# The second edge list of a two-layer graph network in groups of 128 edges instead of 256

## The reference, cut to what matters

```
h_fwd, h_rev = h @ W_forward.T, h @ W_reverse.T                      # 3125 x 64
messages = h_fwd[src] * direction[:, 0:1] + h_rev[src] * direction[:, 1:2]
scores = leaky_relu(einsum('ef,hf->eh', messages, attn_forward[0]), 0.2)   # 4 heads
norm = exp(scores - max) / (segment_sum(exp(scores - max), dst)[dst] + 1e-10)
outs = [segment_sum(messages * norm[:, hd:hd + 1], dst, N) for hd in range(H)]
x = x + stack(outs) + attention(xn)        # then another graph attention with 4 experts
```

## Time and profile before

| | |
|---|---|
| median of 3 runs | 2914.25 us (2913.68 to 2917.84) |
| the profiled execution: its time / its span | 2912.84 us / 2910.9 us |
| busy share of the span: PE, DVE, ACT, POOL | 74%, 57%, 41%, 70% |
| second layer's edge sum | from 1814 us to 2435 us of the span |
| indirect DMAs in it (L2408) | 440 |
| additions of PE's sums in it (L2621) | 220 |
| mean granted TensorE clock | 0.855 |

### The profile page before, as it was taken

One profiled execution on the slowest core, in us unless ns is written; L12 is line 12 of the kernel. 1 busy time (PEld: TensorE's weight loads), 2 busy tenths in 40 slices (PEclk: granted clock), 3 DMA queues, 4 the chain that ended last, 5 costly groups with the idle time before them and its releaser, 6 DMA issues. The chain is left out here.

```text
span 2910.9 us, 34578 instructions
## 1 busy us (share of the span) xinstructions
PE 2167.6 (74%) x10021; PEld 1675.2 (58%) x10021; DVE 1673.6 (57%) x4649; ACT 1187.8 (41%) x3164; POOL 2037.0 (70%) x2064
## 2 busy tenths in 40 slices
PE   0275482277766768999999997688877776999994
PEld 0054361144444447878888876455555455888883
DVE  8937899366679885111000125788887766333236
ACT  0111354155555542222222213699954444344443
POOL 4777777677777776777777633777777773777761
PEclk9996555588888887999999999899987876999997
DMA  2020000533333341356666632322222241111111
GB/s 65 2 63 2 6 3 2 191 105 105 105 104 103 102 98 35 121 163 200 195 197 198 191 105 91 95 53 54 53 52 52 52 49 11 29 32 36 17 19 47
DMA packets 173391, 233.36 MB, mean 80 GB/s; under 512 B 59819, under 2 KB 136622, under 8 KB 172206
## 3 DMA queue, kind: packets, MB, share of 16 engines
q0 software_dynamic: 73664, 103.00, 15.6%
q1 hardware_dynamic: 96504, 117.82, 13.1%
q10 hardware_dynamic: 3062, 10.68, 1.0%
HBM read 192.31 MB, written 39.04 MB: 79 GB/s over the span
## 5 line engine op out<-in xcount | busy, mean ns | idle before, releaser
L831 POOL DMA_INDIRECT slots_gnn<-rec_gnn,slot_row_gnn x782 | 771.3, 986 | 286.4 <-issue 229.9
L2408 POOL DMA_INDIRECT arena<-table,rec_gnn x440 | 457.5, 1040 | 161.9 <-issue 124.7
L1222 POOL DMA_INDIRECT rows_gnn<-support,xT x416 | 401.2, 964 | 132.7 <-issue 110.9
L1266 PE MATMUL banks<-rows_gnn,one_hot 128*128 128x256 f32 x832 | 304.3, 483 | 199.9 <-DMA rows_gnn<-support,xT 174.9
L1266 PEld LDWEIGHTS banks<-rows_gnn,one_hot 128*128 128x128 f32 x832 | 163.1, 228 | 322.8 <-DMA rows_gnn<-support,xT 183.8
L2986 POOL DMA_INDIRECT source_rows<-table_g,source_router x256 | 245.7, 960 | 78.0 <-issue 63.1
L2507 PE MATMUL banks<-weighted,one_hot 128*128 128x260 f32 x880 | 268.7, 458 | 3.0 <-DVE weighted L2604 2.0
L1871 ACT ACTIVATE hidden_private<-banks,b_private 128x256 f32<-128x256 f32 x256 | 107.3, 470 | 354.3 <-PE banks L1829 354.3
L1829 PE MATMUL banks<-slot_xT,w_private 128*128 128x256 f32 x1024 | 228.2, 381 | 1.7 <-DVE slot_xT L1885 1.7
L1841 PE MATMUL banks<-w_private,hidden_private 128*128 128x256 f32 x1024 | 226.1, 379 | 0.0
L2507 PEld LDWEIGHTS banks<-weighted,one_hot 128*128 128x128 f32 x880 | 188.2, 224 | 61.0 <-issue 27.0
(11 more groups left out here) (576 smaller groups left out, 3976.0 us busy)
## 6 DMA issues: line engine op xcount, KB each, us to landing
w_private<-in_w1p SPq DMA_DIRECT2D x32, 1024.0 KB
w_private<-in_w2p SPq DMA_DIRECT2D x32, 1024.0 KB, 7.6
slots_gnn<-rec_gnn,slot_row_gnn POOLq DMA_INDIRECT x782, 2.1
slot_x<-zero_rows ACTq DMA_DIRECT2D x8, 1024.0 KB, 11.2
slot_rows<-slot_x SPq DMA_DIRECT2D x32, 256.0 KB, 7.0
slot_y<-slot_out SPq DMA_DIRECT2D x32, 256.0 KB, 2.2
arena<-table,rec_gnn POOLq DMA_INDIRECT x440, 2.6
rows_gnn<-support,xT POOLq DMA_INDIRECT x416, 2.7
```

Of the source, the lines that this page charges most:

```text
L831: pool.indirect_dma_start(e.slots, bass.IndirectOffsetOnAxis(e.rows[:, j:j + 1], 0), e.rec[:, j, :], None)\
L1222: pool.indirect_dma_start(e.rows_in[:, k, :], None, table, bass.IndirectOffsetOnAxis(row, 0))\
L1266: mm = pe.matmul(bank_of(k // per), hot[:, k, :], e.rows_in[:, row, :], start=k % per == 0, stop=k % per == per - 1)
L2408: pool.indirect_dma_start(c.raw[:, t % RAW_RING, :], None, c.table1, bass.IndirectOffsetOnAxis(row, 0))\
```

## The change

The second list takes groups of 128. It has 416 tiles in 52 rounds. Each tile has its own sum and its own addition: four matmuls of a half go to banks 0 to 3, each with `start` and `stop`, and the next half uses the same four banks again. A new semaphore, `tiles_added1`, counts additions. PE's matmul for tile n waits until addition n-4 is done. DVE makes eight additions a round; each waits for the one before. `add_half(i, 0)` moves up, from behind `late_dve` to directly behind `rescale`, and `scale_v` moves ahead of `add_half(i-1, 1)`. `load_tiles` reads 8 numbers every round, behind `add_half(i-1, 1)`. The attention's output takes two node tiles a round from round 29, so that it ends by round 41. The ring has 64 tiles instead of 72. The POOL part of `attend_stage` waits until all engines have met behind the table stage, not only for the stores.

```diff
-RAW_RING = 72
+RAW_RING = 64
@@ late_dve
-        elif T + 4 <= i < 2 * T + 4:
-            t = i - T - 4
-            dve.wait_ge(self.y_ready, t + 1)
+        elif i >= T + 4:
+            for t in range(2 * (i - T - 4), min(2 * (i - T - 3), T)):
+                dve.wait_ge(self.y_ready, t + 1)
@@ half_sums
             for k in range(HALF * h, HALF * h + HALF):
-                mm = pe.matmul(c.bank[:, k // per, 0:AGG], hot[:, k, :], val[:, k, :, :].rearrange("p h f -> p (h f)"),
-                               start=k % per == 0, stop=k % per == per - 1)
+                n = i * RING + k
+                if n >= HALF:
+                    pe.wait_ge(added, n - HALF + 1)
+                mm = pe.matmul(c.bank[:, k % HALF, 0:AGG], hot[:, k, :], val[:, k, :, :].rearrange("p h f -> p (h f)"),
+                               start=True, stop=True)
@@ rescale
             dve.wait_ge(step, ch.n)
+            if i:
+                dve.wait_ge(added, i * RING)
@@ add_half
             dve.wait_ge(used, 2 * i + h + 1)
-            for k in range(half_groups):
-                g = half_groups * h + k
-                dve.wait_ge(step, ch.n)
-                mark(dve.tensor_tensor(tile_of(i, g), c.bank[:, g, 0:AGG], tile_of(i, g), ALU.add))
+            for g in range(HALF * h, HALF * h + HALF):
+                if i or g:
+                    dve.wait_ge(added, i * RING + g)
+                if g == 0:
+                    dve.wait_ge(step, ch.n)
+                dve.tensor_tensor(tile_of(i, g), c.bank[:, g % HALF, 0:AGG], tile_of(i, g), ALU.add).then_inc(added, 1)
@@ DVE's round
             weigh(i, 0)
+            if 2 <= i <= T + 1:
+                mix.scale_v(dve, i - 2)
             if i:
                 add_half(i - 1, 1)
+            load_tiles(i)
             if more:
                 scaled = forward(i + 1)
-            if 2 <= i <= T + 1:
-                mix.scale_v(dve, i - 2)
-            if i % TURN == 0:
-                load_tiles(i)
             one_hots(i, 1)
@@
             rescale(i)
+            add_half(i, 0)
             if 1 <= i <= T:
                 mix.variances(dve, ch, i - 1)
@@
             mix.late_dve(dve, i)
-            add_half(i, 0)
             if more:
                 shift(i + 1)
@@ attend_stage, POOL
-        pool.wait_ge(c.table_stored, 16 * c.table_stores)
+        pool.wait_ge(met, 4 * (met_n - 1))
@@ build
-        e1 = Edges(c, "gnn1", EDGES, a["dst"], a["src"], a["edge_attr_2"], top, rounds=True)
+        e1 = Edges(c, "gnn1", EDGES, a["dst"], a["src"], a["edge_attr_2"], top, group=P, rounds=True)
```

More of the change, by code:

```diff
@@ L39 @@
 PARTS_IN_FLIGHT = FLIGHT // HALF
-BODY_GROUPS = RING * P // GROUP
+ROOM_WORDS = 1736
 NEG = -1.0e30
@@ L185, in hold_records @@
         if then_slots:
-            self.room = c.sb(ctx, f"rec_{self.name}", [P, max(self.per, self.tiles) * self.width])
+            self.room = c.sb(ctx, f"rec_{self.name}", [P, max(self.per * self.width, self.tiles * self.width, ROOM_WORDS)])
             self.rec = self.room[:, 0:self.per * self.width].rearrange("p (j w) -> p j w", w=self.width)
@@ L1185, in _ @@
           .then_inc(e.slot_in, 16)
-TURN = 3
 def tiles_of_groups(c, engine, e, first, n):
@@ L2327, in late_pe @@
             mm.then_inc(self.mat2_ready, 1)
-        elif T + 3 <= i < 2 * T + 3:
-            t = i - T - 3
-            if t == 0:
-                pe.wait_ge(self.mat2_out, 1)
-            if t >= 2:
-                pe.wait_ge(self.y_out, t - 1)
-            out = self.raw[:, t % 2, 0:D]
-            for k in range(KD):
-                pe.matmul(out, self.c.xT[:, k, t * P:(t + 1) * P], self.mat2[:, k, :], start=k == 0, stop=False)
-            pe.matmul(out, self.c.ones[0:1, 0:P], self.bo[:], start=False, stop=True).then_inc(self.y_ready, 1)
+        elif i >= T + 3:
+            for t in range(2 * (i - T - 3), min(2 * (i - T - 2), T)):
+                if t == 0:
+                    pe.wait_ge(self.mat2_out, 1)
+                if t >= 2:
+                    pe.wait_ge(self.y_out, t - 1)
+                out = self.raw[:, t % 2, 0:D]
+                for k in range(KD):
+                    pe.matmul(out, self.c.xT[:, k, t * P:(t + 1) * P], self.mat2[:, k, :], start=k == 0, stop=False)
+                pe.matmul(out, self.c.ones[0:1, 0:P], self.bo[:], start=False, stop=True).then_inc(self.y_ready, 1)
 class TableWeights:
@@ L2422, in sum1_stage @@
     steps = e.tiles // RING
-    assert steps >= 2 * T + 4
+    assert steps >= T + 4 + (T + 1) // 2
     tops = c.sb(ctx, "round_tops", [P, HEADS1, steps])
@@ L2439, in sum1_stage @@
     met = c.met
-    per = GROUP // P
-    half_groups = HALF // per
+    added = c.sem(ctx, "tiles_added1")
     ring_rounds = RAW_RING // RING
```

11 lines of the change are left out of this document (5 added, 6 removed).

## The result

The changed kernel takes 3019.17 us (median of 4 runs, 3017.03 to 3021.21), the kernel before in the same series 2913.99 us (4 runs, 2913.68 to 2917.84). The ratio is 1.0354, with a 95% interval of 1.0339 to 1.037. The profiled execution has a span of 3019.5 us at a granted clock of 0.842. So the kernel is slower, by 105 us where I had forecast 70.

A forecast was written before the change was run, and what follows sets the result against it. DVE was taken to bound attention rounds, POOL's gathers later ones; after the change DVE bounds both, at 13.3 and 12.3 us a round. The stage goes from 592.0 to 662 us, so 2912.8 + 70 = 2983 us, range 2930 to 3020.

The forecast's parts named there:

- tile numbers: DVE reads 8 tile numbers each round behind a chain of waits: +0.30 us a round, between 0 and 0.63.
- PE's wait in the later rounds: DVE waits for PE's sums of half 1 in later rounds: 1.2 us a round, bounds 0.1 to 1.8.
- rival 2: Dearer: PE's sums at 1.2 GHz every later round, tile numbers 0.63, attention rounds 0.4 more; +110, 3023 us; chance 11%.
- The four chained additions: On DVE, four additions waiting for each other take 2.04 us against 0.90 for two: +1.14 per half, +2.28 a round.
- rival 3: Each of DVE's four new additions costs only 0.33 us, 1.32 a round for 2.28; +21, 2934 us; chance 4%.
- The move: Half 0's additions move up on DVE: +0.42 us a round of uncovered spread wait, +0.10 for depending on the rescaling.
- PE in attention rounds: The 13.3 us attention round held no term for DVE waiting for PE's sums; that wait was charged to later rounds.
- The chain through ACT: In attention rounds DVE's 0.77 us a round of waiting for ACT's exponential goes; variances coming 2 us later cost nothing.
- At nothing: Costed at nothing: 24 fewer gathers, the ring of 64 tiles, attend_stage's wait; longer group_tile and slot loading under 1 us together.
- Ends: Stage pieces outside the two long stretches: round 0 to 1 11.5 us, rounds 26 to 29 38.3, the end 8.9.
- Rival 1: Cheaper by half: PE stays at 2.4 GHz, tile-number read hidden; periods 13.0 and 10.9, +30, 2943 us; chance 17%.
- Rival 4: POOL stays the bound, additions fit into DVE's waits, gathers end 32 us earlier; faster, 2881 us; chance 4%.

The follow-up runs named there:

- additions spread out: The changed kernel with DVE's work reordered so that another operation stands between any two additions of a running sum; 2883.27 us, 0.9891 of the kernel before.
- PE kept busy: The changed kernel with useless matmuls on PE, four or three a round, between the turn of the top score and its spread; 2984.62 us.
- pairs with 416 tiles: The kernel before, with groups of 256, four additions a round and the old order, but 416 tiles in 52 rounds instead of 440 tiles; 2871.88 us.

## Why the forecast was right in kind and short in size

The forecast was slower, 2983 us in a range of 2930 to 3020; the time is 3019.2, 0.8 us inside its upper end. That it lies inside is luck in part: the bounds that I worked out for the range were those of the tile numbers and of PE's wait in the later rounds, and the larger part of the error came from a wait in attention rounds that I had at nothing. It comes close to rival 2 (3023 us), and by rival 2's means, PE's sums, but not by its tile numbers, and with more of it in attention rounds and less in the later ones (periods 14.35 and 12.84 for 14.0 and 13.2). The kernel with the additions spread out shows that nothing forced the loss.

**The four chained additions.** Right. They take 2.14 us by the timeline, 2.06 to the next instruction (2011.89 to 2013.95), where I had 2.04. An addition on its own takes 0.34 to the next, where I had worked out 0.33. The Trainium skill, page VectorE: DVE Perf Modes, section on the DRAIN, has a semaphore after each operation cost nothing extra. These runs differ, and the measurement decides: a semaphore on which the very next addition waits costs 0.23 us. They agree with the page where the next instruction doesn't wait for it (0.34 us for each of four additions in buffers of their own) or where another operation stands between (0.34 in the additions spread out). So rival 3, which had each new addition at 0.33 us, had the wrong kind of addition in view.

**The move.** My terms for it on DVE were 0.42 us of uncovered spread and 0.10 of dependence on the rescaling, 0.52 a round. DVE alone needs 13.27 us with the move (sums ahead of the spread) and 12.73 without, so 0.54: the sum was right. The split was not. From the rescaling to the first addition it is 0.56 us (2011.33 to 2011.89); with the additions put back the next instruction comes 0.35 behind the rescaling, so the dependence costs 0.21 for my 0.10, within its bounds. From the diagonal to `shift` it is 0.69 us in the round shown (2015.79 to 2016.48), 0.79 in the mean of attention rounds and 0.86 later, where I had 0.89 for both. Less the 0.47 that were covered before, 0.32 is left for my 0.42. In attention rounds the edit that puts the additions back is worth 14.35 - 12.74 = 1.61 us a round: 0.54 of DVE's own, 0.88 that DVE waits for PE's sums, and 0.19 that the next paragraph takes up.

**PE in attention rounds: the step that failed.** I wrote that the sums of half 1 "start when the score is spread and are waited for by DVE", and charged a wait of 1.2 us to later rounds alone. In attention rounds I took nothing and gave no reason; before, it had been 3.7 us in six rounds, at a clock of 0.95. But the four additions, 2.06 us, stand ahead of the diagonal, and PE's queue holds the spread ahead of the sums. PE was idle for some 3.5 us, and in 22 of 25 rounds the sums then took 2.82 to 3.84 us instead of 2.02. DVE's waits for the sums came to 22.1 us in 25 rounds, 0.88 a round. My 13.3 us and 0.88 make 14.2; measured are 14.35. Of the last 0.17 some 0.1 is `shift` waiting for the spread (4.7 us, against 2.0 in the kernel with the sums ahead of it); the rest I can't assign. Without the waits for the sums it is 13.27 us in that kernel, 13.46 with PE kept busy, and 13.3 to 13.5 in the three rounds of the changed kernel itself that have none: the sum for DVE alone held. The attention rounds are 26.7 us over my 332, two thirds of the error of the stage (701.5 for 662).

**PE in later rounds.** The mechanism was right and the size short: 38.2 us in 22 rounds are 1.74 each, for the 1.2 I took; with it 12.3 becomes 12.84. That is 12 us, and it is rival 2's 1.8. The clock there was 0.76, not 0.81, and PE waited 2.8 us a round for the diagonal, the same idle time as above; I had counted only that DVE comes 0.34 us earlier.

**The chain through ACT.** Right: the 0.77 us a round are gone, no wait for ACT is left in attention rounds.

**Tile numbers.** I took 0.30 us; `forward` is held 0.31 us behind the chain of additions (2022.68), 6.8 us in 22 of 25 rounds. Right.

**At nothing.** Gathers: DVE's waits for them are gone, POOL waits for the ring, 70.3 us, and ends later than before. Right, as long as DVE is the slower one. The pairs with 416 tiles show what the 24 gathers are worth otherwise, 43 us. The wait of `attend_stage`: right by the rows. The ring of 64 alone wasn't tried.

**Ends.** Round 0 to 1 took 12.64 us for 11.5, rounds 26 to 29 37.8 for 38.3, the tail 9.8 for 8.9.

**Rivals.** Rival 1 (13.0 and 10.9 us, 2943) is, near enough, the kernel with the additions put back: 12.74 and 10.82 us, 2932.5. Rival 4, POOL as the bound and the kernel faster, needs a period of DVE under 10.76 over the whole stage; the change was far from it. The additions spread out come near it, 2883.3 us for its 2881, though DVE needs 11.55 in the first part: the tiles that POOL gets ahead are worth 10.13 in the second. That I took no notice of in the text.

## What to carry to other kernels

When work moves up in an engine's order, ask not only what that engine waits for, but who waits for what now comes behind it, and what is queued behind that wait on the other engine; here a moved block of 2 us cost 0.54 us a round on DVE and 0.88 more through PE, and in attention rounds neither the lateness nor the lower clock of PE's sums would have cost that by itself. Additions that must keep an order are cheap when something else stands between two of them, so four in a row are better dealt out over the round. A price found for a move in one grouping (8 us here) is no price in another (87): slack that covers a small delay need not cover a larger one. And an order that beats the two kernels compared need not be the best: of all the kernels here the pairs with 416 tiles are the fastest, where the input allows them.

## What was unexpected of the hardware

- The same eight matmuls take 1.92 and 3.71 us within one round, the slow one behind 3.42 us of idle time, at a granted clock of 0.54. Behind 1.86 us of it, with useless matmuls ahead, they take 2.02 in 19 of 25 rounds. Work that nobody needs made the kernel 34.5 us faster. The idle time alone doesn't tell: behind 1.15 us, with the additions put back, 18 of 25 are slow, and behind 3.29 us two of 25 are not.
- An addition that waits for the one just ahead of it on DVE starts about 0.23 us later than an instruction that does not (2.06 less 0.34 for three steps is 0.57, against 0.34), while the addition's own duration stays at 420 to 428 ns: the price shows as idle time of the successor and in no duration.
- The kernel before took 2914 us on some chips and 4246 and 4285 us on two others. Attention rounds in which DVE hardly waits kept their median there to 0.1 us, those of the pairs with 416 tiles did not (12.29 for 10.84), and ratios between kernels did not carry over: additions put back was 1.0056 of the kernel before here, and 0.9972 there.
